# Six of batch 0's eight weight units computed with seven half-size products instead of plain tiles, with the sums and differences on GpSimd

## What is computed

```
x = x + fq(layernorm(x)) @ fq(ctx)                # 2 batches, 1024 tokens, 2048 x 2048 per batch
h = layernorm(x)                                  # over the 2048 features
base = h @ W_base.T + b_base                      # 2048 x 2048
lora = sum over e of w[t,e] * (h @ A[e].T) @ B[e].T * 2    # 8 experts, rank 16, top 2
x = x + base + lora
```

## Time and the profile before

| | |
|---|---|
| median of 3 runs | 1009.75 us (1008.69 to 1011.86) |
| profiled execution | 1009.48 us, of it 1007.8 us span |
| PE busy | 966.3 us, 96% |
| DVE busy | 780.7 us, 77% |
| ACT busy | 433.9 us, 43% |
| GpSimd (POOL) busy | 133.6 us, 13% |

### The profile page before, as it was taken

The page is one execution under the profiler, slowest core; times in us unless marked ns, Lnnn a source line. Parts: engine busy times, 40 slices in busy tenths (PEclk is TensorE's granted clock), DMA queues, the critical chain, the costliest instruction groups (busy, mean ns, idle before and its releaser), DMA issues.

```text
span 1007.8 us, 15099 instructions
## 1 busy us (share of the span) xinstructions
PE 966.3 (96%) x5875; PEld 524.8 (52%) x5875; DVE 780.7 (77%) x1430; ACT 433.9 (43%) x468; POOL 133.6 (13%) x168
## 2 busy tenths in 40 slices
...
GB/s 376 354 155 284 253 249 284 205 328 315 207 134 70 92 183 189 283 234 154 201 235 196 178 237 154 69 141 289 206 142 125 69 152 113 81 136 78 111 74 31
DMA packets 62311, 185.65 MB, mean 184 GB/s; under 512 B 6896, under 2 KB 19488, under 8 KB 56096
## 3 DMA queue, kind: packets, MB, share of 16 engines
...
...
## 4 chain that ended last, share of the span: by engine, by line
PE 78%; DVE 3%; DMA 2%; ACT 1%; issue 0%; DVEq 0%; ACTq 0%
PE pair L1768 31%; PE pair L1791 28%; PE pair L1623 13%; PE pair L1747 4%; PE pair L1737 1%; DMA spread<-scratch 1%; DMA scratch<-w_max 1%; DMA w_r<-in_w_n 1%; PE pair L1803 1%; DVE w_p L1187 0%; ACT w_r L774 0%; PE pair L1713 0%; PE pair L1638 0%; DVE cent L1243 0%; DVE cent L1282 0%
## 5 line engine op out<-in xcount | busy, mean ns | idle before, releaser
L1768 PE MATMUL pair<-x2p,w_p 128*128 128x512 f16 x1536 | 336.7, 379 | 0.2 <-DVE w_p L1187 0.2
L1768 PEld LDWEIGHTS pair<-x2p,w_p 128*128 128x128 f16 x1536 | 150.2, 98 | 181.1 <-DVE w_p L1187 0.7
L1623 PE MATMUL pair<-q1T,ctx_q 128*128 128x342 f16 x1536 | 232.8, 312 | 12.1 <-DVE xt L977 5.7
L1623 PEld LDWEIGHTS pair<-q1T,ctx_q 128*128 128x128 f16 x1536 | 149.4, 98 | 89.8 <-issue 10.7
L1791 PE MATMUL pair<-x2p,w_slot 128*128 128x512 f16 x744 | 163.8, 379 | 0.0
L801 ACT ACTIVATE sq<-pair,lsc 128x512 f32<-128x512 f32 x64 | 43.7, 682 | 236.7 <-PE pair L1747 200.8
L1567 POOL TENSOR_SCALAR ctx_u<-ctx_f,par 128x512 uint8<-128x512 f32 x128 | 114.9, 911 | 148.2 <-DMA ctx_f<-in_ctx 91.8
L1791 PEld LDWEIGHTS pair<-x2p,w_slot 128*128 128x128 f16 x744 | 72.9, 98 | 87.7
L829 ACT ACTIVATE w_slot<-w_q,usc 128x1024 f16<-128x1024 f32 x32 | 36.5, 1146 | 92.1 <-DVE usc L1402 27.2
L1791 PE MATMUL pair<-x2p,x2p 128*128 128x512 f16 x336 | 74.3, 379 | 0.0
L977 DVE SCALAR_TENSOR_TENSOR xt<-pair,par,xt 128x342 f32<-128x342 f32 (+1 forms) x96 | 53.7, 565 | 16.0 <-PE pair L1623 15.6
(11 more groups left out here) (214 smaller groups left out, 1078.4 us busy)
## 6 DMA issues: line engine op xcount, KB each, us to landing
ctx_f<-in_ctx SPq DMA_DIRECT2D x32, 1024.0 KB, 7.2
xt<-in_xT SPq DMA_DIRECT2D x32, 512.0 KB, 4.5
w_r<-in_w_n SPq DMA_DIRECT2D x32, 512.0 KB, 7.0
w_f<-in_w_t SPq DMA_DIRECT2D x32, 512.0 KB, 5.5
w_q<-in_w_t SPq DMA_DIRECT2D x32, 512.0 KB, 5.1
...
rows<-in_x SPq DMA_DIRECT2D x15, 1024.0 KB, 9.2
x_kept<-xt ACTq DMA_DIRECT2D x16, 512.0 KB, 4.8
```

The source lines that it names most:

```text
L1623: ins = M.matmul(bank[at % RING][:, 0:W3], ctx_q[n % NQ][:, k, :], q1T[b][:, k, c * W3:(c + 1) * W3], start=(k == 0), stop=(k == KT - 1))
L1768: M.matmul(base_bank(m)[:, :], w_p[j % 2][wh][:, k, :], x2p[0][:, k, xh, t], start=(k == 0 and q == 0), stop=(k == KT - 1 and q == 2))
```

## The change

Batch 0 keeps the plain form for two units (i = 0 and 1, eight tiles). Its other six units use seven products each, as batch 1's eight units do. Units are now counted by v from 0 to 13: v = 0 to 5 are of batch 0, v = 6 to 13 of batch 1.

- Batch 0's differences: eight pairs of tiles are read back from `x_kept`, which now holds both batches. They are worked on in pairs beside the eight plain tiles, and lie in `x2p[1]`, over batch 1's operands. GpSimd makes the four subtractions of every pair, and the low part of three pairs; DVE makes the low part of five.
- Batch 1's own operands go to DRAM in the first stage (`x2_kept`, by ACT's queue). Its differences are made in 16 pieces of 4 x 256 columns beside units 0 to 5, three pieces in a unit: ACT's queue loads a piece and stores it, GpSimd makes the four subtractions and the low part, ACT the high part and a scaled copy.
- At the turn (v = 5 to 6) the seven right operands are loaded again, each as soon as unit 5's product that reads its place is done (`load_xb`): 14 DMAs.
- The four sums of W's quarters move from DVE to GpSimd, in all 14 units.
- `out_base` takes x from DRAM in two instructions everywhere, and stands further ahead of its take.
- The bounds' way through DRAM goes from GpSimd's queue to SP's (`bounds_out`, `bounds_in`). The bounds of `b` are taken from all of `b` at once.
- The left operands go round 8 places, and product 3's and 4's takes come before product 2's.

```diff
-PLAIN = NC * JT
+PLAIN_UNITS = 2
+PLAIN = NC * PJ
+UNIT = [(0, i) for i in range(PLAIN_UNITS, UNITS)] + [(1, i) for i in range(UNITS)]
+TURN = UNITS - PLAIN_UNITS
...
+            def load_xb(p):
+                t, k0, half = X_OF[p]
+                sp.wait_ge(product, PRODUCTS * (TURN - 1) + p + 1)
...
+                for h in range(2):
+                    sp.dma_start(t[:, k0:k0 + HALF, h, half], src[k0:k0 + HALF, :, h, half].rearrange("j p t -> p j t")).then_inc(xb_landed[p], 16)
...
+            def piece_high(e):
+                act.wait_ge(xd_ready, UNITS + e + 1)
+                if e:
+                    act.wait_ge(xd_stored, 64 * e)
+                A.activation(piece_out(0), piece_in(), ACT.Copy, scale=xsT[:, 1:2])
+                A.activation(piece_in(), piece_in(), ACT.Copy, scale=xsT[:, 1:2]).then_inc(xd_hi, 1)
...
-            for j in range(JT):
-                roundtrip(w_max[:, :], w_bound, j + 1, 4, w_out, w_in, 16 * (j + 1))
+            def differences(e, f):
+                G.tensor_tensor(f[:, 1, 1, :], f[:, 1, 1, :], f[:, 0, 1, :], ALU.subtract).then_inc(xd_step, 1)
...
+            def pieces(v, n):
+                pool.wait_ge(xd_landed[2], 32 * (e + 1))
+                differences(UNITS + e, piece_in().rearrange("p (s a) t -> p s a t", a=2))
+                pool.wait_ge(xd_hi, UNITS + e + 1)
+                G.tensor_tensor(piece_out(1), piece_in(), piece_out(0), ALU.subtract).then_inc(xd_lo_pool, 1)
...
+            for v in range(TOTAL - 1):
+                quarter_sum(v + 1, 0)
+                pieces(v, 0)
+                quarter_sum(v + 1, 1)
+                quarter_sum(v + 1, 2)
+                quarter_sum(v + 1, 3)
+                pieces(v, 1)
+                pieces(v, 2)
```

More of the change, by code:

```diff
@@ L316, in xattn_ffn @@
         lora_taken = sem("lora_taken")
-        xd_landed = sem("xd_landed")
+        b_max = sem("b_max")
+        us_result = sem("us_result")
+        xsT_ready = sem("xsT_ready")
+        x2_stored = sem("x2_stored")
+        xd_landed = [sem(f"xd_landed{s}") for s in range(3)]
         xd_step = sem("xd_step")
@@ L623, in _ @@
[L623 to L649 removed]
+            store(2)
@@ new lines, in _ @@
+            w_sum(6, 1)
+            s_high(0, 0)
+            s_high(0, 1)
+            load_pair(7)
+            lora_of(5)
+            pair_high(7)
+            w_sum(7, 0)
+            s_high(0, 2)
+            w_sum(7, 1)
+            lora_of(6)
+            s_high(0, 3)
+            s_high(0, 4)
+            s_high(0, 5)
+            lora_of(7)
+            s_high(0, 6)
+            load_piece(0)
+            for v in range(TOTAL):
+                m = PLAIN + 4 * v
+                n = 2 * (PLAIN_UNITS + v + 2)
+                ahead = n + 1 < JT
+                more = v + 1 < TOTAL
+                if more:
+                    s_high(v + 1, 0)
+                if ahead:
+                    w_sum(n, 0)
+                p1_copy(v)
+                if more:
+                    s_high(v + 1, 1)
+                if ahead:
+                    w_sum(n, 1)
@@ L1520, in _ @@
-            b2_of(0)
-            for i in range(UNITS):
-                more = i + 1 < UNITS
-                if more:
-                    unit_scale(i + 1)
-                if i:
-                    quarter_out(i - 1, 3)
-                else:
-                    plain_out(PLAIN - 1)
-                if not more:
+            out_base(2)
+            pair_low(1)
+            plain_out(1)
+            w_scale_of(2)
+            b_of(2)
+            lora_scale_of(2)
+            w_low(2)
+            w_bound_of(3)
@@ new lines, in _ @@
+            pair_low(6)
+            s_low(0, 1)
+            out_base(6)
+            plain_out(5)
+            w_scale_of(6)
+            pair_low(7)
+            s_low(0, 2)
+            out_base(7)
+            w_bound_of(7)
+            plain_out(6)
+            s_low(0, 3)
+            s_low(0, 4)
+            w_scale_of(7)
+            unit_scale(1)
+            s_low(0, 5)
+            plain_out(7)
+            b2_of(0)
+            s_low(0, 6)
+            for v in range(TOTAL):
+                m = PLAIN + 4 * v
+                n = 2 * (PLAIN_UNITS + v + 2)
+                ahead = n + 1 < JT
+                if v:
+                    quarter_out(v - 1, 3)
+                if v + 1 == TOTAL:
@@ new lines, in _ @@
+                s_low(v + 1, 0)
+                s_low(v + 1, 1)
+                out_base(m)
+                quarter_out(v, 0)
+                out_base(m + 1)
+                s_low(v + 1, 2)
+                if ahead:
+                    w_bound_of(n)
+                out_base(m + 2)
+                take(v, 1)
+                s_low(v + 1, 3)
+                if ahead:
+                    w_scale_of(n)
+                    w_bound_of(n + 1)
+                take(v, 2)
+                quarter_out(v, 1)
```

986 lines of the change are left out of this document (567 added, 419 removed).

## The result

After: 1212.34 us median of 4 runs (1209.31 to 1217.03); before, on the same chip: 1009.71 (1008.69 to 1011.86). The ratio is 1.2008, 95% interval 1.1963 to 1.2052. The forecast was 998.4 us, 981 to 1026. One execution of a later run (e_before_xk0, 1474 us at a granted clock of 0.66) was in a slower state of the chip and is left out.

The account below looks back on a forecast made before the run. The prediction took PE's own work as the bound. From 1009.5 us it took 31.1 for fewer matmuls and added 13 for the port, 4 for the plain tiles and unit 0, 3 for the turn: 998.4 us, range 981 to 1026.

Parts of the forecast that it names:

- Part 1: Second stage, six units: seven products in place of four plain tiles save PE 5.2 us a unit, 31.1 us.
- Part 2: Units 0 to 4: GpSimd and DVE exclude each other at one SBUF port, 42.2 us a unit; costs 13 us.
- chain of the pieces: Rival, units 0 to 4: hand-overs among POOL, ACT and its queue make a unit 41.3 to 45 us; 1016.5 us; chance 0.26.
- Part 3: Eight plain tiles and unit 0: port work of 72 us just fits in 73; costs 4 us, between 0 and 15.
- Part 4: The turn, units 5 to 6: fourteen reload DMAs and ordinary traffic take 64 of 67 us; costs 3 us, between 0 and 12.
- Part 5: First-stage stores, DVE's reduction of all of `b` and the bounds' way over SP stay hidden behind matmuls; costs nothing.

Follow-up runs that it names:

- e_before_xk0: The kernel before with only the first-stage stores of batch 0's x to x_kept by ACT's queue added, without those of x2_kept: 1024.3 us, ratio 1.0151.
- e_nlt_tiny_pool: The changed kernel without loads of pieces 1 to 15 and the bounds' way through DRAM, GpSimd's two-input instructions in the second stage over 8 columns: 1061.4 us.

## Why the prediction was wrong

**What held.** Part 1: seven products are 5.2 us a unit less, the units from v = 7 on last 38.8 to 38.9 us and PE is their bound. The duration of GpSimd's instructions: 1024 elements take 2.12 to 2.35 us undisturbed, 2.1 to 2.3 ns an element, and the prediction took 2.2. This is also what the Trainium skill states (GPSIMD Engine Reference, Performance versus the Vector engine: 4497 ns for 2048), and the trace agrees within a tenth: GpSimd's instructions of 2048 elements took 4.06 us. That DVE's 512-element instructions would stretch to over 2 us: they did.

**Part 2, 13 us for the port: mis-sized, and by a wrong sum.** It held the port's demand, 42.2 us, against the unit, 38.9. But what DVE loses at the port is added to all that DVE does, also to what needs no port (takes, bounds, scales). Its own sum had the right figure for DVE alone, 31.9 us (30.9 measured); with 17 us lost that is 47.8 us of DVE, 8.9 over PE, not 3.4. (This was seen in the kernel without loads and bounds' way, where the hand-overs alone hold a unit at 47.5 us too, so it is DVE's bound and not the port's price.) About two fifths of the loss are paid by small instructions which the prediction counted at nothing, as the 128x1 row shows. The rule in the Trainium skill (SBUF — State Buffer, Who interferes with whom) names no least size, and the trace agrees. In the kernel as it is most of this is hidden behind a longer chain:

**The rival "chain of the pieces" was the likelier one and was mispriced.** It had the right engines and order, at 41.3 to 45 us a unit with 0.26. The five units last 51.6 to 63.2. Wrong in it: the issue, 0.33 for 0.65 us; row sums counted at their length, while they wait for loads of W's rows (23.5 us in the units, of 91.2 in the trace) with the pieces behind them; and a load that starts only when the buffer's last user is through. Taken out one after another, the runs give 36 us to that load's round trip, 31 more to the pieces' work, and 16 to the bounds' way and 11 to the rest, the four together 94.8.

**Part 3, 4 us for the plain tiles and unit 0: the step that failed most, 101.9 us.** It weighed port time against time (72 us in 73), and no engine was the bound: DVE was busy 54%. It also read the earlier trace rows as PE being in time by 0.2 us, where PE already waited 0.2. What was never laid out is which instruction stands behind which. The runs put in the place of the 4 us: pairs 40 us, the bounds' way 24, the place of two loads in SP's queue 12. The remaining 26 us were not taken apart: without the three chains ACT still waits 50.7 us for loads of W's rows there, but no run removed those.

**Part 4, 3 us for the turn: 16.2.** The prediction summed the transfer and gave each product 33 us "from its load's earliest issue". The loads were not issued then. The last one's place was free when unit 5's last product ended at about 871.4 us, but in SP's queue it stands behind stores and the loads of rows:

```profile
866.26 5.34 PE L2088 MATMUL pair<-x2p,w_slot 128*128 128x512 f16 x24
909.14 1.12 SPq L622 DMA_DIRECT2D x2p<-xd_kept  x2
921.55 8.23 PE L2088 MATMUL pair<-x2p,w_slot 128*128 128x512 f16 x24 [9.42 <-DMA x2p<-xd_kept]
```

38 us went by before the issue, 12 from it to PE's start, and PE waited 9.42 us for it. No run moved this load. With the reload kept and GpSimd's and the loads' share gone (e_nlt_tiny_pool) the turn costs 2.4 us, so the transfer itself was priced about right. Without the pieces it is 7.7: some 8.5 us come with the pieces, and the rest shows only where the reload and GpSimd's full sums meet.

**Part 5, at nothing: 18 us and 24 us.** That the stores "in the first stage hide behind its matmuls" was said of a stage whose DMA share was 0.63 to 0.77, from ACT's issue time alone. The bounds' way over SP was called 1 to 3 us once; behind waits for stores and loads it costs the tiles and unit 0 24 us. The first stage's 18 us go with the stores: in the kernel before they alone cost 21.

The six costs were each taken small because each engine had room. The range would have had to hold a case in which the hand-written order as a whole does not fit: none was in it.
